# Layer norm computed in two halves, and the output bias moved from the norm into the attention

## The chip, the cores and the metric

The kernel runs on one core of a Trainium2 chip. The core has TensorE (PE: matmuls, weight loads shown apart as PEld), VectorE (DVE), ScalarE (ACT), GpSimd (POOL) and SyncE (SP, here DMA issues only). The metric is the device time of one execution in microseconds, as the median of several runs. A profile is one further execution.

## The reference, cut to what matters

Four layers work on x of 8 sequences x 256 tokens x 128 features. Each layer adds a gated cross attention and a gated feed-forward network, both fed by a layer norm of x:

```python
def _layernorm(x, axis=-1, eps=1e-05):
    m = jnp.mean(x, axis=axis, keepdims=True)
    v = jnp.var(x, axis=axis, keepdims=True)
    return (x - m) / jnp.sqrt(v + eps)
...
x = x + jnp.tanh(g_xattn[1]) * _L1_xattn_ref(_layernorm(x, axis=-1), ctx_768, L1_xattn_Wq, ..., L1_xattn_bo)
x = x + jnp.tanh(g_ffn[1]) * _L1_ffn_ref(_layernorm(x, axis=-1), L1_ffn_router_w, ...)
```

Every attention ends with `out @ Wo + bo`. So x receives, per layer, the gate times the attention's output and the gate times the bias `bo`. The norm in front reads x without either. Layer 0 has 16 heads of 8 features and a quantised feed-forward network, layers 1 and 3 have 16 heads of 64, layer 2 has 8 heads of 128 whose keys span all 2048 tokens, and layers 1 to 3 have expert networks with a router.

## The kernel before, in words

All 2048 tokens stay in SBUF as `x_res` (`M.x`): 128 partitions x 16 token tiles (`NT`) x 128 features. The program is a row of blocks. Each block gives every engine a list of instructions, and at a block's end all five engines meet at a barrier, so a block lasts as long as its slowest engine. Inside a block each engine works strictly in the written order and waits on semaphores; there is no scheduler and no planner.

The norm is a block of its own (`layernorm`, used six times: ahead of the four attentions and of the feed-forward networks of layers 0 and 3). The expert blocks of layers 1 and 2 (`sparse_ffn`) hold the same code at their start, so there are eight norms. In a norm

- DVE computes the statistics of the 16 tiles (L422, `BATCH_NORM_STATS2`), then seven small instructions on 128x16 numbers (L425 to L433) that end in variance plus epsilon, `ln_var_eps`;
- POOL raises this to the power -1/2 (L447, `ln_rstd`; L2291 in the expert blocks);
- DVE normalises the 16 tiles (L436; L2536 in the expert blocks), PE transposes each tile (L457), ACT copies four tiles at a time out of PSUM (L468, L470), and DVE forms the f16 remainder (L442, four instructions);
- ahead of an attention, POOL then adds the gated bias to all of `x_res` (L450) once all 16 tiles are normalised.

`attention` (layers 1 and 3) runs over 16 heads of 4 blocks of 512 queries. Heads 0 to 13 are a hardware loop of seven rounds, heads 14 and 15 are written out; the last one prepares no further head. Per block DVE does for each of two halves: reciprocal of the denominators (L1112), then two instructions that add the weighted output to `x_res` (L1122, the first waits for the reciprocal through the semaphore `rden_done`), and besides the remainders of the queries (L1088) and of the probabilities (L1128) and two maxima (L1098). PE writes both output halves (L969) into the same PSUM bank, so it writes the next one only when DVE has read the last. `attention_wide` (layer 2) does this with other tiles (L1516 adds to `x_res`; POOL shares the remainders of the probabilities, L1446, with DVE, L1494). In layer 0, `attention_small_heads` does not touch `x_res`; `gathered_projection` behind it does.

Of the kernel before, what the change touches and what calls it, by code (L numbers as in the profile page):

```python
# [28 lines left out]
P = 128  # L29
D = 128  # L30
# [26 lines left out]
def build(nc, d, out):  # L57
    with ExitStack() as ctx:
        M = persistent(nc, ctx)
        prepare(nc, M, d)  # L60
        for n in range(4):
            layernorm(nc, M, 2 * n, split=True, plain=False, bias=n)
# [10 lines left out]
            layernorm(nc, M, 2 * n + 1, split=n > 0, plain=True, bias=None)  # L73
# [326 lines left out]
def layernorm(nc, M, k, split, plain, bias):  # L400
# [4 lines left out]
    with ExitStack() as ctx:  # L405
# [8 lines left out]
        stat0 = seen * (NT + 5)  # L414
# [3 lines left out]
        with nc.Block() as block:  # L418
            @block.vector
            def _(dve):  # L420
                for t in range(NT):
                    nc.vector.bn_stats(st[:, t, :], M.x[:, t, :]).then_inc(s["stat"], 1)  # L422
                dve.wait_ge(s["stat"], stat0 + NT)

                nc.vector.tensor_tensor(a[:], st[:, :, 1], st[:, :, 4], ALU.add).then_inc(s["stat"], 1)  # L425
                nc.vector.tensor_tensor(b[:], st[:, :, 1], st[:, :, 4], ALU.subtract).then_inc(s["stat"], 1)
                nc.vector.tensor_tensor(c[:], st[:, :, 2], st[:, :, 5], ALU.add).then_inc(s["stat"], 1)
                dve.wait_ge(s["stat"], stat0 + NT + 3)
                nc.vector.tensor_scalar(mean[:], a[:], 0.5, None, ALU.mult)
                nc.vector.tensor_tensor(e[:], b[:], b[:], ALU.mult).then_inc(s["stat"], 1)  # L430
                nc.vector.tensor_scalar(c[:], c[:], 1.0 / D, EPS, ALU.mult, ALU.add).then_inc(s["stat"], 1)
                dve.wait_ge(s["stat"], stat0 + NT + 5)
# [41 lines left out]
def attention_small_heads(nc, M):  # L474
# [6 lines left out]
    with ExitStack() as ctx:  # L481
# [41 lines left out]
        with nc.Block() as block:  # L523
            @block.gpsimd
            def _(pool):
# [3 lines left out]
                nc.gpsimd.memset(empty[:, :, D:D + 1], 1.0e6).then_inc(empty_done, 1)  # L529

# [236 lines left out]
def attention(nc, M, layer):  # L767
# [90 lines left out]
    with ExitStack() as ctx:  # L858
# [37 lines left out]

        with nc.Block() as block:
# [178 lines left out]
            def _(pool):  # L1076
# [86 lines left out]
def attention_wide(nc, M, layer):  # L1163
# [9 lines left out]
    with ExitStack() as ctx:  # L1173
# [39 lines left out]

        with nc.Block() as block:
# [224 lines left out]
            def _(pool):  # L1439
                for r in (32, 96):  # L1440
                    nc.gpsimd.memset(K3[r:r + 1, :], 1.0).then_inc(ones_set, 1)

# [25 lines left out]
            def _(dve):  # L1468
# [41 lines left out]
                def add(b, half):  # L1510
                    qb = b % NQ
                    dve.wait_ge(o_ready, b + 1)
                    dve.wait_ge(rden_done, b + 1)
                    for t in (2 * half, 2 * half + 1):
# [655 lines left out]
def sparse_ffn(nc, M, d, layer):  # L2170
# [11 lines left out]
    with ExitStack() as ctx:  # L2182
# [66 lines left out]
        with nc.Block() as block:  # L2249
# [30 lines left out]
            def _(pool):  # L2280
# [9 lines left out]
                pool.wait_ge(var, 1)  # L2290
                nc.gpsimd.tensor_tensor(rstd[:], ve[:], M.neghalf[:], ALU.pow).then_inc(rstd_done, 1)  # L2291
# [472 lines left out]
```

## Time and profile before

| | |
|---|---|
| device time, median of 3 runs (lowest, highest) | 2480.14 us (2479.51, 2485.76) |
| device time of the profiled execution | 2482.54 us |
| its span, first to last instruction | 2480.8 us |
| busy: PE, DVE, ACT, POOL | 82%, 70%, 54%, 21% of the span |
| mean granted TensorE clock | 0.893 of full speed |

The profiled execution took 1.7 us more than its span; what is changed in the span is taken to change the device time by as much. Busy shares are averages over stages of different kinds: in a norm block the span is set by a chain through DVE and POOL, in the attentions by PE or DVE. The span of a chain is read from the timeline, by the start of one instruction and the start of the next that waits for it.

### The profile page before, as it was taken

The numbers are of one execution on the slowest core, as the hardware profiler recorded it, in microseconds if no ns is written. First come the engines' busy times: TensorE is split into PE (matmuls) and PEld (weight loads), VectorE is DVE, ScalarE is ACT, GpSimd is POOL, SyncE is SP. The second block draws the span as 40 slices with busy tenths as digits, with TensorE's granted clock in tenths as the row PEclk, the third lists the DMA queues.
The fourth block names the chain that finished last, engine by engine and source line by source line (L and its number), as shares of the span: only waits on it lengthen the run. The fifth ranks groups of instructions, "written<-read, shape, count | busy, mean of one in ns | idle before, by whom it ended". The sixth has DMA issues, their size and how long they took to land. (4 is left out here: it accounts for less than half of the span.)

```text
span 2480.8 us, 47937 instructions
## 1 busy us (share of the span) xinstructions
PE 2031.9 (82%) x17000; PEld 1395.1 (56%) x17001; DVE 1742.9 (70%) x3576; ACT 1339.0 (54%) x1775; POOL 531.4 (21%) x510
## 2 busy tenths in 40 slices
PE   3699636999984949999999999999547389999677
PEld 3434324888864715555555555556436268888544
DVE  2567365888875457788787877876535468888688
ACT  1247314777753416666666666667335257777321
POOL 2100001000002323434443344435433300000010
PEclk9679766999996959999999999999668689999789
DMA  5311100000004010000000000000211100000000
GB/s 143 57 24 11 23 0 1 0 0 0 0 27 120 19 49 9 9 12 9 12 9 11 11 9 12 9 11 4 84 54 40 40 1 0 0 0 0 1 22 24
DMA packets 94870, 53.74 MB, mean 22 GB/s; under 512 B 43517, under 2 KB 88808, under 8 KB 94358
## 3 DMA queue, kind: packets, MB, share of 16 engines
q1 hardware_dynamic: 86516, 42.51, 7.3%
q0 software_dynamic: 3584, 6.36, 0.8%
q10 hardware_dynamic: 4610, 2.71, 0.5%
q8 instruction: 104, 1.70, 0.3%
q14 instruction: 56, 0.46, 0.1%
HBM read 30.16 MB, written 13.75 MB: 18 GB/s over the span
## 5 line engine op out<-in xcount | busy, mean ns | idle before, releaser
L1446 POOL TENSOR_TENSOR aw_p_lo<-aw_p,aw_p_hi 128x512 f16<-128x512 f32 x256 | 303.1, 1184 | 499.6 <-ACT aw_p_hi L1400 499.5
L1482 DVE TENSOR_REDUCE aw_max_part<-ps 128x1 f32<-128x512 f32 x512 | 349.8, 686 | 77.2 <-PE ps L1275 74.4
L1398 ACT ACTIVATE aw_p<-ps 128x1024 f32<-128x1024 f32 x256 | 262.3, 1024 | 260.2 <-PE ps L1307 260.1
L1324 PE MATMUL ps<-ctx_hi_lo,aw_p_hi 128*128 128x194 f16 x2048 | 290.8, 247 | 1.2 <-DVE aw_p_lo L1494 0.7
L1494 DVE TENSOR_TENSOR aw_p_lo<-aw_p,aw_p_hi 128x512 f16<-128x512 f32 x256 | 267.5, 1045 | 22.0 <-ACT aw_p_hi L1400 22.0
L1327 PE MATMUL ps<-ctx_hi_lo,aw_p_lo 128*128 128x97 f16 x2048 | 279.4, 207 | 0.0
L1400 ACT ACTIVATE aw_p_hi<-ps 128x1024 f16<-128x1024 f32 x256 | 260.5, 1018 | 0.0
L1275 PE MATMUL ps<-ctxT_hi,aw_queries 96*128 96x512 f16 x512 | 204.1, 400 | 36.0 <-DVE aw_max_part L1482 35.4
L1327 PEld LDWEIGHTS ps<-ctx_hi_lo,aw_p_lo 128*128 128x128 f16 x2048 | 200.4, 98 | 26.1
L1324 PEld LDWEIGHTS ps<-ctx_hi_lo,aw_p_hi 128*128 128x128 f16 x2048 | 199.7, 98 | 5.0 <-issue 4.0
L1302 PE MATMUL ps<-aw_queries,aw_keys 128*128 128x512 f16 x512 | 194.5, 380 | 0.3 <-ACT aw_p_hi L1400 0.3
L1303 PE MATMUL ps<-aw_queries,aw_keys 128*128 128x512 f16 x512 | 193.9, 379 | 0.0
L1040 ACT ACTIVATE at_p<-ps 128x1024 f32<-128x1024 f32 x128 | 131.1, 1024 | 102.9 <-PE ps L946 102.9
L1098 DVE TENSOR_REDUCE at_neg_max<-ps 128x2 f16<-128x512 f32 x256 | 174.3, 681 | 6.0 <-PE ps L925 5.6
L1122 DVE SCALAR_TENSOR_TENSOR x_res<-ps,at_rden,x_res 128x128 f32<-128x128 f32 x520 | 158.6, 347 | 9.2
L447 POOL TENSOR_TENSOR ln_rstd<-ln_var_eps,neg_half 128x16 f32<-128x16 f32 x6 | 17.6, 2932 | 687.3 <-DVE ln_var_eps L433 653.2
L969 PE MATMUL ps<-C,u_out 97*128 (+1 forms) x1040 | 160.2, 276 | 5.1 <-DVE x_res L1122 5.1
L1128 DVE TENSOR_TENSOR at_p_lo<-at_p,at_p_hi 128x1024 f16<-128x1024 f32 x128 | 155.6, 1216 | 7.9 <-ACT at_p_hi L1042 7.7
L969 PEld LDWEIGHTS ps<-C,u_out 97*128 97x128 f32 x1040 | 136.2, 191 | 11.6 <-DVE x_res L1122 8.3
L956 PE MATMUL ps<-at_p_hi,ctx_hi_lo 128*128 128x256 f16 x512 | 140.9, 275 | 1.1 <-DVE at_p_lo L1128 1.1
L944 PE MATMUL ps<-at_q_hi,ctxT_hi 97*128 97x256 f16 x512 | 141.6, 277 | 0.0
L945 PE MATMUL ps<-at_q_hi,ctxT_lo 96*128 96x256 f16 x512 | 141.5, 276 | 0.0
(377 smaller groups left out, 4687.3 us busy)
## 6 DMA issues: line engine op xcount, KB each, us to landing
sf_weights_raw<-in_L_w SPq DMA_DIRECT2D x24, 256.0 KB, 4.1
slot_scratch<-at_empty_rows SPq DMA_DIRECT2D x16, 260.0 KB, 8.1
sf_fetched<-slot_scratch SPq DMA_DIRECT2D x16, 260.0 KB, 3.0
sf_weights_raw<-in_L_w SPq DMA_DIRECT2D x8, 512.0 KB, 3.8
x_norm<-result_scratch SPq DMA_DIRECT2D x8, 256.0 KB, 4.2
aw_queries<-aw_queries SPq DMA_DIRECT2D x32, 64.0 KB, 1.9
aw_queries<-aw_q_lo SPq DMA_DIRECT2D x32, 64.0 KB, 2.0
raw<-in_L_q SPq DMA_DIRECT2D x3, 512.0 KB, 10.4
```

The costliest lines, as they stand in the source:

```text
L969: ins = nc.tensor.matmul(ps[:, BANKS[b], t * (CW + 1):(t + 1) * (CW + 1)], M.U[:, upar, (2 * half + t) * P:(2 * half + t + 1) * P], C[:, s ...
L1098: nc.vector.tensor_reduce(nmax[:, par, 2 * k:2 * k + 2], ps[:, BANKS[b], :].rearrange("p (t k) -> p t k", t=2), AX.X, ALU.max, negate=True ...
L1275: nc.tensor.matmul(ps[:, bank, :], S1[0:DC, b % 4, t * P:(t + 1) * P], M.ct_hi[0:DC, kb * QB:(kb + 1) * QB], start=True, stop=True).then_i ...
L1302: nc.tensor.matmul(o, K1[:, ks], S1[:, c, :], start=True, stop=False)
L1303: nc.tensor.matmul(o, K2[:, ks], S2[:, c, :], start=False, stop=False)
L1324: nc.tensor.matmul(ps[:, bank, at:at + 2 * VW - 2], p_hi[:, n % 3, cols], M.cv[:, kt, 0:2 * VW - 2], start=kt == 0 and t % 2 == 0, stop=False,
L1327: ins = nc.tensor.matmul(ps[:, bank, at:at + DA], p_lo[:, n % 3, cols], M.cv[:, kt, 0:DA], start=False, stop=kt == NT - 1, skip_group_chec ...
L1398: nc.scalar.activation(p[:, n % 2, :].rearrange("p (b q) -> p b q", b=2), s, ACT.Exp, scale=1.0 / QS).then_inc(p_done, 1)
L1400: nc.scalar.activation(p_hi[:, n % 3, :].rearrange("p (b q) -> p b q", b=2), s, ACT.Exp, scale=1.0 / QS).then_inc(hi_done, 1)
L1446: nc.gpsimd.tensor_tensor(p_lo[:, n % 3, QB:], p[:, n % 2, QB:], p_hi[:, n % 3, QB:], ALU.subtract).then_inc(lo_b, 1)
L1482: nc.vector.tensor_reduce(mpart[:, b % 2, k:k + 1], ps[:, bank, :], AX.X, ALU.max).then_inc(m_done, 1)
L1494: nc.vector.tensor_tensor(p_lo[:, n % 3, 0:QB], p[:, n % 2, 0:QB], p_hi[:, n % 3, 0:QB], ALU.subtract).then_inc(lo_a, 1)
```

## The change

Three things change.

1. In every norm the 16 tiles are handled as two halves of 8 (`H = NT // 2`). DVE does statistics and the seven small instructions for tiles 0 to 7, then for tiles 8 to 15, and only then normalises; POOL computes the power in two instructions of 128x8 instead of one of 128x16, each as soon as its half's variance is there. The first 8 tiles are normalised after the first power, the others after the second.
2. The bias is no longer added in the norm. POOL adds it at the start of the attention that follows: in layer 0 behind its memsets, in layers 1 and 3 as POOL's only work, in layer 2 behind the memsets of the keys.
3. In layers 1 to 3 a new semaphore `bias_added` holds DVE's first addition to `x_res` back until the bias is in. The wait stands in the code of every such addition.

```diff
-def layernorm(nc, M, k, split, plain, bias):
+def layernorm(nc, M, k, split, plain):
...
+                for i in range(2):
+                    half, stats = slice(i * H, (i + 1) * H), stat0 + i * (H + 5)
+                    for t in range(i * H, (i + 1) * H):
+                        nc.vector.bn_stats(st[:, t, :], M.x[:, t, :]).then_inc(s["stat"], 1)
+                    dve.wait_ge(s["stat"], stats + H)
+                    nc.vector.tensor_tensor(a[:, half], st[:, half, 1], st[:, half, 4], ALU.add).then_inc(s["stat"], 1)
...
+                    nc.vector.scalar_tensor_tensor(ve[:, half], e[:, half], 0.25, c[:, half], ALU.mult, ALU.add
+                                                   ).then_inc(s["var"], 1)
                 for t in range(NT):
...
-                nc.vector.scalar_tensor_tensor(ve[:], e[:], 0.25, c[:], ALU.mult, ALU.add).then_inc(s["var"], 1)
-                dve.wait_ge(s["rstd"], seen + 1)
-                for t in range(NT):
+                    if t % H == 0:
+                        dve.wait_ge(s["rstd"], 2 * seen + t // H + 1)
                     nc.vector.tensor_scalar(M.xn[:, t, 0:D], M.x[:, t, :], mean[:, t:t + 1], rstd[:, t:t + 1],
                                             ALU.subtract, ALU.mult).then_inc(s["norm"], 1)
...
             def _(pool):
-                pool.wait_ge(s["var"], seen + 1)
-                nc.gpsimd.tensor_tensor(rstd[:], ve[:], M.neghalf[:], ALU.pow).then_inc(s["rstd"], 1)
-                if bias is not None:
-                    pool.wait_ge(s["norm"], (seen + 1) * NT)
-                    nc.gpsimd.tensor_tensor(M.x[:], M.x[:],
-                                            M.obias[:, bias:bias + 1, :].to_broadcast([P, NT, D]), ALU.add)
+                for i in range(2):
+                    half = slice(i * H, (i + 1) * H)
+                    pool.wait_ge(s["var"], 2 * seen + i + 1)
+                    nc.gpsimd.tensor_tensor(rstd[:, half], ve[:, half], M.neghalf[:, half], ALU.pow
+                                            ).then_inc(s["rstd"], 1)
...
@@ attention (layers 1 and 3), POOL and DVE @@
+                nc.gpsimd.tensor_tensor(M.x[:], M.x[:], M.obias[:, layer:layer + 1, :].to_broadcast([P, NT, D]),
+                                        ALU.add).then_inc(bias_added, 1)
...
                     v = ps[:, BANKS[at[0]], 0:2 * (CW + 1)].rearrange("p (t w) -> p t w", t=2)
+                    dve.wait_ge(bias_added, 1)
                     dve.wait_ge(rden_done, blk * 2 + half + 1)
```

`attention_wide` gets the same addition and the same wait (behind its two waits `o_ready` and `rden_done`), `attention_small_heads` the addition without a semaphore, and `sparse_ffn` the same two halves as `layernorm`.

The order of DVE's instructions in a norm, here the one of layer 0, before (`ln_` tiles belong to the norm, `ps` is PSUM; names in brackets are the semaphores an instruction waits for):

```order
L422 BN_STATS ln_stats<-x_res 128x6 x16
L425 TENSOR_TENSOR ln_a<-ln_stats 128x16 [waits ln_stat]
L426 TENSOR_TENSOR ln_b<-ln_stats 128x16
L427 TENSOR_TENSOR ln_c<-ln_stats 128x16
L429 TENSOR_SCALAR ln_mean<-ln_a 128x16 [waits ln_stat]
L430 TENSOR_TENSOR ln_e<-ln_b 128x16
L431 TENSOR_SCALAR ln_c<-ln_c 128x16
L433 SCALAR_TENSOR_TENSOR ln_var_eps<-ln_e,ln_c 128x16 [waits ln_stat]
L436 TENSOR_SCALAR x_norm<-x_res,ln_mean,ln_rstd 128x128 [waits ln_rstd]
L436 TENSOR_SCALAR x_norm<-x_res,ln_mean,ln_rstd 128x128 x15
L442 TENSOR_TENSOR x_normT_lo<-ps,x_normT_hi 128x512 [waits ln_hi] x4
```

The same place in the changed kernel, from the second half's statistics on (the first half's eight rows, which stand ahead, read the same as the first eight here):

```order
L424 BN_STATS ln_stats<-x_res 128x6 x8
L426 TENSOR_TENSOR ln_a<-ln_stats 128x8 [waits ln_stat]
L427 TENSOR_TENSOR ln_b<-ln_stats 128x8
L429 TENSOR_TENSOR ln_c<-ln_stats 128x8
L431 TENSOR_SCALAR ln_mean<-ln_a 128x8 [waits ln_stat]
L432 TENSOR_TENSOR ln_e<-ln_b 128x8
L433 TENSOR_SCALAR ln_c<-ln_c 128x8
L436 SCALAR_TENSOR_TENSOR ln_var_eps<-ln_e,ln_c 128x8 [waits ln_stat]
L441 TENSOR_SCALAR x_norm<-x_res,ln_mean,ln_rstd 128x128 [waits ln_rstd]
L441 TENSOR_SCALAR x_norm<-x_res,ln_mean,ln_rstd 128x128 x7
L441 TENSOR_SCALAR x_norm<-x_res,ln_mean,ln_rstd 128x128 [waits ln_rstd]
L441 TENSOR_SCALAR x_norm<-x_res,ln_mean,ln_rstd 128x128 x7
```

Between the first half's variance and the first normalisation DVE now has the second half's 15 instructions (8 of statistics, 7 small ones), and there is a second wait in the middle of the normalisation.

```order
L444 UNCONDITIONAL_BRANCH
L447 ISA
L447 TENSOR_TENSOR ln_rstd<-ln_var_eps,neg_half 128x16 [waits ln_var]
L450 TENSOR_TENSOR x_res<-x_res,out_bias 128x2048 [waits ln_norm]
L418 UNCONDITIONAL_BRANCH
L1075 UNCONDITIONAL_BRANCH [waits barrier_Pool_Activation_PE_DVE_SP_gather]
L897 UNCONDITIONAL_BRANCH
```

The same place in the changed kernel:

```order
L449 UNCONDITIONAL_BRANCH
L454 ISA
L454 TENSOR_TENSOR ln_rstd<-ln_var_eps,neg_half 128x8 [waits ln_var] x2
L418 UNCONDITIONAL_BRANCH
L1082 UNCONDITIONAL_BRANCH [waits barrier_Pool_Activation_PE_DVE_SP_gather]
L1089 TENSOR_TENSOR x_res<-x_res,out_bias 128x2048
L904 UNCONDITIONAL_BRANCH
```

The addition has moved from the norm's side of the barrier to the attention's side, and waits for nothing there.

DVE in the loop of the attention of layer 1, one half block and the query and maximum work behind it, before:

```order
L1112 RECIPROCAL at_rden<-ps 128x2 [waits at1_job_ready1]
L1122 SCALAR_TENSOR_TENSOR x_res<-ps,at_rden,x_res 128x128 [waits at1_rden_done]
L1122 SCALAR_TENSOR_TENSOR x_res<-ps,at_rden,x_res 128x128
L1086 REGISTER_ALU
L1088 TENSOR_TENSOR at_q_lo<-ps,at_q_hi 96x512 [waits at1_q_hi_done]
L1093 REGISTER_ALU
L1098 TENSOR_REDUCE at_neg_max<-ps 128x2 [waits at1_job_ready2]
```

The same place in the changed kernel:

```order
L1121 RECIPROCAL at_rden<-ps 128x2 [waits at1_job_ready1]
L1132 SCALAR_TENSOR_TENSOR x_res<-ps,at_rden,x_res 128x128 [waits at1_rden_done,at1_bias_added]
L1132 SCALAR_TENSOR_TENSOR x_res<-ps,at_rden,x_res 128x128
L1095 REGISTER_ALU
L1097 TENSOR_TENSOR at_q_lo<-ps,at_q_hi 96x512 [waits at1_q_hi_done]
L1102 REGISTER_ALU
L1107 TENSOR_REDUCE at_neg_max<-ps 128x2 [waits at1_job_ready2]
```

Nothing is reordered, but the first addition behind each reciprocal now has two waits. The wait for `rden_done` becomes an EVENT_SEMAPHORE of its own between the reciprocal and the addition.

## Rows read from the trace of the kernel before

**Rows 1.** The page: span, then busy us, share and instructions by engine.

```profile
span 2480.8 us, 47937 instructions
PE 2031.9 (82%) x17000; PEld 1395.1 (56%) x17001; DVE 1742.9 (70%) x3576; ACT 1339.0 (54%) x1775; POOL 531.4 (21%) x510
```

**Rows 2.** Busy time in layer 3's attention: length; PE, PEld, DVE, ACT, POOL; clock; DMA.

```profile
2007.00:2329.00 322.00, 317.74 (x2700) 262.06 (x2698) 281.11 (x634) 230.81 (x310) 0.00 (x0) 1.00 0.00 0
```

**Rows 3.** Timeline, norm of layer 0: start, length (us), engine, line, what, count, [idle before<-releaser].

```profile
90.48 3.19 DVE L422 BATCH_NORM_STATS2 ln_stats<-x_res 128x6 f32<-128x128 f32 x16 [0.30 <-PEq L193]
...
94.48 0.18 DVE L433 SCALAR_TENSOR_TENSOR ln_var_eps<-ln_e,ln_c 128x16 f32<-128x16 f32 x1
94.74 2.94 POOL L447 TENSOR_TENSOR ln_rstd<-ln_var_eps,neg_half 128x16 f32<-128x16 f32 x1 [75.50 <-DVE ln_var_eps L433]
97.72 4.19 DVE L436 TENSOR_SCALAR x_norm<-x_res,ln_mean,ln_rstd 128x128 f32<-128x128 f32 x16 [3.06 <-POOL ln_rstd L447]
...
101.84 2.47 DVE L442 TENSOR_TENSOR x_normT_lo<-ps,x_normT_hi 128x512 f16<-128x512 f32 x4
102.00 4.50 POOL L450 TENSOR_TENSOR x_res<-x_res,out_bias 128x2048 f32<-128x2048 f32 x1 [4.31 <-DVE x_norm L436]
...
106.82 0.59 PE L556 MATMUL ps<-ctxT_hi,w0k_hi 97*128 97x512 f16 x1 [4.38 <-PEq L418]
```

**Rows 4.** Two lines' instructions: ns min/median/max, first and last start.

```profile
L447 POOL TENSOR_TENSOR ln_rstd<-ln_var_eps,neg_half x6: 2912/2937/2947, 94.7 to 2333.3; 128x16 f32<-128x16 f32 x6
...
L450 POOL TENSOR_TENSOR x_res<-x_res,out_bias x4: 4495/4496/4497, 102.0 to 1973.6; 128x2048 f32<-128x2048 f32 x4
```

**Rows 5.** Timeline, the norm ahead of the attention of layer 1.

```profile
373.22 2.95 POOL L447 TENSOR_TENSOR ln_rstd<-ln_var_eps,neg_half 128x16 f32<-128x16 f32 x1 [34.11 <-issue]
376.20 4.20 DVE L436 TENSOR_SCALAR x_norm<-x_res,ln_mean,ln_rstd 128x128 f32<-128x128 f32 x16 [6.75 <-POOL ln_rstd L447]
```

**Rows 6.** Timeline, layer 1's expert block: its power and the first scatter of tokens.

```profile
739.90 2.92 POOL L2291 TENSOR_TENSOR sf_rstd<-sf_var_eps,neg_half 128x16 f32<-128x16 f32 x1 [2.95 <-DVE sf_var_eps L2533]
...
760.78 1.30 POOL L2297 DMA_INDIRECT slot_scratch<-x_norm,sf_slot_at  x1 [17.97 <-DVE sf_slot_at L2607]
```

**Rows 7.** Timeline, layer 2's attention: POOL and DVE on SBUF tiles together.

```profile
957.30 1.16 POOL L1446 TENSOR_TENSOR aw_p_lo<-aw_p,aw_p_hi 128x512 f16<-128x512 f32 x1 [2.25 <-ACT aw_p_hi L1400]
957.45 1.56 DVE L1494 TENSOR_TENSOR aw_p_lo<-aw_p,aw_p_hi 128x512 f16<-128x512 f32 x1
```

**Rows 8.** Timeline, layer 0's quantised network: one scaling over 2048 columns.

```profile
317.13 1.29 DVE L1665 TENSOR_SCALAR qf_tmp<-x_normT,qf_inv_x 128x2048 f32<-128x2048 f32 x1
```

**Rows 9.** Timeline, one block near the end of layer 1's attention.

```profile
703.51 0.17 DVE L1112 RECIPROCAL at_rden<-ps 128x2 f32<-128x2 f32 x1 [0.34 <-PE ps L969]
...
703.72 0.61 DVE L1122 SCALAR_TENSOR_TENSOR x_res<-ps,at_rden,x_res 128x128 f32<-128x128 f32 x2
...
704.24 1.22 DVE L1128 TENSOR_TENSOR at_p_lo<-at_p,at_p_hi 128x1024 f16<-128x1024 f32 x1
...
704.50 0.52 PEld L969 LDWEIGHTS ps<-C,u_out 97*128 97x128 f32 x4
```

**Rows 10.** Waits from 420 to 710 us: us in total, times, longest.

```profile
DVE at_rden L1112 <- PE ps L969: 15.6, 58, 0.3
```

**Rows 11.** Timeline of DVE where layer 1's attention ends (unrolled, L1107's wait between).

```profile
715.46 0.68 DVE L1098 TENSOR_REDUCE at_neg_max<-ps 128x2 f16<-128x512 f32 x1
716.29 0.17 DVE L1112 RECIPROCAL at_rden<-ps 128x2 f32<-128x2 f32 x1
716.49 0.61 DVE L1122 SCALAR_TENSOR_TENSOR x_res<-ps,at_rden,x_res 128x128 f32<-128x128 f32 x2
```

**Rows 12.** Timeline, last additions of layer 3's attention.

```profile
2326.49 0.61 DVE L1122 SCALAR_TENSOR_TENSOR x_res<-ps,at_rden,x_res 128x128 f32<-128x128 f32 x2
2327.15 0.71 PE L969 MATMUL ps<-C,u_out 97*128 97x129 f32 x4 [0.91 <-DVE x_res L1122]
```

**Rows 13.** Timeline of DVE: the first addition to x in layer 1's attention.

```profile
416.19 0.61 DVE L1122 SCALAR_TENSOR_TENSOR x_res<-ps,at_rden,x_res 128x128 f32<-128x128 f32 x2
```

More of the change, by code:

```diff
@@ L61, in build @@
         for n in range(4):
-            layernorm(nc, M, 2 * n, split=True, plain=False, bias=n)
+            layernorm(nc, M, 2 * n, split=True, plain=False)
             if n == 0:
@@ L72, in build @@
                 continue
-            layernorm(nc, M, 2 * n + 1, split=n > 0, plain=True, bias=None)
+            layernorm(nc, M, 2 * n + 1, split=n > 0, plain=True)
             if n == 0:
@@ L413, in layernorm @@
         M.norms += 1
-        stat0 = seen * (NT + 5)
+        stat0, H = seen * (NT + 10), NT // 2
         splits0 = M.splits
@@ L434, in _ @@
-                dve.wait_ge(s["rstd"], seen + 1)
-                for t in range(NT):
+                for i in range(2):
[4 more added lines that the diff above has]
+                    nc.vector.tensor_tensor(a[:, half], st[:, half, 1], st[:, half, 4], ALU.add).then_inc(s["stat"], 1)
+                    nc.vector.tensor_tensor(b[:, half], st[:, half, 1], st[:, half, 4], ALU.subtract
+                                            ).then_inc(s["stat"], 1)
+                    nc.vector.tensor_tensor(c[:, half], st[:, half, 2], st[:, half, 5], ALU.add).then_inc(s["stat"], 1)
+                    dve.wait_ge(s["stat"], stats + H + 3)
+                    nc.vector.tensor_scalar(mean[:, half], a[:, half], 0.5, None, ALU.mult)
+                    nc.vector.tensor_tensor(e[:, half], b[:, half], b[:, half], ALU.mult).then_inc(s["stat"], 1)
+                    nc.vector.tensor_scalar(c[:, half], c[:, half], 1.0 / D, EPS, ALU.mult, ALU.add
+                                            ).then_inc(s["stat"], 1)
+                    dve.wait_ge(s["stat"], stats + H + 5)
+                    nc.vector.scalar_tensor_tensor(ve[:, half], e[:, half], 0.25, c[:, half], ALU.mult, ALU.add
+                                                   ).then_inc(s["var"], 1)
@@ L1212, in is_unit @@
             return 0 <= n < NU
+        bias_added = sem("bias_added")
         with nc.Block() as block:
@@ L1441, in _ @@
                     nc.gpsimd.memset(K3[r:r + 1, :], 1.0).then_inc(ones_set, 1)
+                pool.wait_ge(ones_set, 2)
+                nc.gpsimd.tensor_tensor(M.x[:], M.x[:], M.obias[:, layer:layer + 1, :].to_broadcast([P, NT, D]),
+                                        ALU.add).then_inc(bias_added, 1)
                 def lows(n):
@@ L2289, in _ @@
                                    allow_small_or_imprecise_dtypes=True).then_inc(consts, 1)
-                pool.wait_ge(var, 1)
-                nc.gpsimd.tensor_tensor(rstd[:], ve[:], M.neghalf[:], ALU.pow).then_inc(rstd_done, 1)
+                for i in range(2):
+                    half = slice(i * NT // 2, (i + 1) * NT // 2)
+                    pool.wait_ge(var, i + 1)
+                    nc.gpsimd.tensor_tensor(rstd[:, half], ve[:, half], M.neghalf[:, half], ALU.pow
+                                            ).then_inc(rstd_done, 1)
                 for k in range(K):
@@ L2529, in _ @@
-                V.tensor_scalar(mean[:], a[:], 0.5, None, ALU.mult)
-                V.tensor_tensor(e2[:], b[:], b[:], ALU.mult).then_inc(stat, 1)
-                V.tensor_scalar(c[:], c[:], 1.0 / D, EPS, ALU.mult, ALU.add).then_inc(stat, 1)
-                dve.wait_ge(stat, NT + 5)
-                V.scalar_tensor_tensor(ve[:], e2[:], 0.25, c[:], ALU.mult, ALU.add).then_inc(var, 1)
-                dve.wait_ge(rstd_done, 1)
-                for t in range(NT):
+                H = NT // 2
+                for i in range(2):
+                    half, stats = slice(i * H, (i + 1) * H), i * (H + 5)
+                    for t in range(i * H, (i + 1) * H):
+                        V.bn_stats(st[:, t, :], M.x[:, t, :]).then_inc(stat, 1)
+                    dve.wait_ge(stat, stats + H)
+                    V.tensor_tensor(a[:, half], st[:, half, 1], st[:, half, 4], ALU.add).then_inc(stat, 1)
+                    V.tensor_tensor(b[:, half], st[:, half, 1], st[:, half, 4], ALU.subtract).then_inc(stat, 1)
+                    V.tensor_tensor(c[:, half], st[:, half, 2], st[:, half, 5], ALU.add).then_inc(stat, 1)
+                    dve.wait_ge(stat, stats + H + 3)
+                    V.tensor_scalar(mean[:, half], a[:, half], 0.5, None, ALU.mult)
+                    V.tensor_tensor(e2[:, half], b[:, half], b[:, half], ALU.mult).then_inc(stat, 1)
+                    V.tensor_scalar(c[:, half], c[:, half], 1.0 / D, EPS, ALU.mult, ALU.add).then_inc(stat, 1)
+                    dve.wait_ge(stat, stats + H + 5)
+                    V.scalar_tensor_tensor(ve[:, half], e2[:, half], 0.25, c[:, half], ALU.mult, ALU.add
+                                           ).then_inc(var, 1)
```

22 lines of the change are left out of this document (6 added, 16 removed).

## The prediction

> **What bounds the kernel now.** I read the page first, for the shares, then the timeline of each norm block, then busy time by stretch and the timeline in the attentions that get a new wait. No engine bounds the whole: PE is busy 82%, DVE 70%, POOL 21% [rows 1]. So every edit is priced in its own stage.
>
> In a norm block the end is set by one chain. In layer 0 [rows 3]: DVE's statistics start at 90.48 and end at 93.67; seven small instructions end with the variance at 94.66; POOL's power runs from 94.74 to 97.68 with DVE idle (3.06 us); DVE normalises from 97.72 to 101.91; the remainders end at 104.31. Then only POOL works: its bias addition, held back until the last tile is normalised, runs from 102.00 to 106.50, and the next block's first matmul follows at 106.82. Two costs are to be seen there: an exposed power of 2.94 us, and 106.50 - 104.31 = 2.19 us in which all engines wait for the addition. Power and addition last the same everywhere, 2937 and 4496 ns in the median [rows 4].
>
> In the attentions of layers 1 and 3 PE is the bound: 317.7 us busy of 322 at full granted clock [rows 2]. A block repeats every 5.04 us, and DVE waits for PE in each, 15.6 us in 58 blocks or 0.27 us a block [rows 10].
>
> **The change, part by part.**
>
> Bias out of the norm. Four norms had it. Each block now ends with DVE: 4 x 2.19 = 8.8 us gained. The additions go into the attentions. In layer 1 the norm's work ends 6.7 us (4.2 + 2.5) after 376.20, the barrier takes about 0.5, so POOL adds from about 383.4 to 387.9; DVE's first addition to x comes at 416.19 [rows 5, 13], 28 us later, so the new wait holds nothing back. Nor should the addition slow DVE: beside it in the norm, four remainders (one input from PSUM, one from SBUF) took 2.47 us, 0.62 each [rows 3], and DVE's work at an attention's start reads PSUM too. Bounds: 0, or 4.5 us for each of the four were DVE held for all of it; I take 0. POOL has nothing urgent behind the addition.
>
> The new wait. In layers 1 and 3 there are 16 x 4 + 1 = 65 pairs of output halves, so 130 times per layer the wait for the reciprocal becomes an EVENT_SEMAPHORE ahead of the addition. The trace has this pattern ahead of L1112: the maximum ends at 716.14, the reciprocal starts at 716.29, 0.15 us later; with the wait carried by the instruction itself the gap is 716.46 to 716.49, 0.03 [rows 11]. So it costs 0.11 us. Not below 0, since it waits for what was waited for before; up to 0.15. In the steady blocks there is cover for just that. The additions end at 704.33 and PE's next weight load for that bank starts at 704.50 [rows 9], while where PE does wait for the additions it follows 0.05 behind (2327.10 to 2327.15) [rows 12]: slack 0.12 against 0.11. Over a block DVE loses 0.22 against its idle 0.27. So the loop stays at 5.04. If the cover fails, each 0.01 us beyond it costs 60 x 2 x 0.01 = 1.2 us. In the last head DVE and PE hand one bank to and fro [rows 12], and the wait shows: of its last ten projections I count seven on the chain, 7 x 2 x 0.11 = 1.5 us lost (0 to 20 x 0.11 = 2.2). In layer 2 each first addition had two waits already, so no sequencer instruction is added: 0, at most 64 x 0.11 = 7.
>
> Two halves. The power of 8 columns is not in the trace. Bounds: half of 2.94, or all of it. POOL's subtraction of 512 columns takes 1.16 us [rows 7] and its addition of 2048 takes 4.50 [rows 4], 2.17 ns a column and 0.05 fixed, so POOL is paid by the column: 0.05 + 2.89 / 2 = 1.50. The halved statistics take 1.6 us, the small instructions 1.0 as before, since at 128x16 they are all start-up. In layer 0's times: first variance 93.1, first power 93.2 to 94.7, second statistics and variance done at 95.7, second power wants 95.8 to 97.3, and DVE can normalise from 95.7. With nothing in its way it ends at 95.7 + 4.19 = 99.9 instead of 101.91: 2.0 us gained.
>
> But then the second power runs beside the normalisation. The rows nearest to that: POOL's subtraction from 957.30 to 958.46, DVE's from 957.45 to 959.01, 1.56 us for what would take 0.61 by the 1.22 of twice the size [rows 7, 9]. DVE came second and ended 0.55 after POOL: it had stood still. Does the normalisation, with one tensor input, use what they compete for? Scaling 2048 columns within SBUF took 1.29 us [rows 8], 0.63 ns a column, where DVE's subtraction with two inputs takes 1.22 for 1024 [rows 9], 1.19 ns. It takes two columns at a time, so I read it as using the second way in and out too. Then the first tile goes 95.7 to 96.0, the power to 97.5, fifteen tiles 97.5 + 14 x 0.26 + 0.34 = 101.4: 0.5 gained. If DVE holds POOL off instead, the eight tiles end at 97.8, the power at 99.3, and the other eight at 101.5: the same. I take 0.5 of 0.5 to 2.0, the rows nearest saying so. The statistics go at one column a time and are not held. Seven norms: 7 x 0.5 = 3.5 us. In the expert blocks it passes on, since the first scatter at 760.78 hangs on the norm through DVE [rows 6]. The eighth, ahead of layer 1's attention, differs: its power starts at 373.22 for a reason that is POOL's own ("issue", where layer 0's row names DVE), and DVE stands idle for 6.75 us [rows 3, 5]. There the powers end at 374.7 and 376.2; DVE, held by the second, starts at 376.25 instead of 376.20: 0, or 1.45 gained if it isn't held.
>
> The Trainium skill has this as a rule (SBUF — State Buffer, "Who interferes with whom"): a VectorE `tensor_scalar` in a two-port mode, or an instruction with two SBUF inputs against a GpSimd one that reads SBUF, excludes GpSimd's instruction for its whole length, and whoever comes first blocks the other. By that rule each norm gains 0.5; without it 2.0. The trace agrees for two inputs (the 1.56 us); for the normalisation no row shows it.
>
> **Sum.** -8.8 (barrier) - 3.5 (halves) + 1.5 (last heads) = -10.8 us. The profiled execution is 2482.54 with 1.7 outside its span, so 2471.7 for one like it; the median of the runs shown is 2.4 lower, and that is what is compared: 2480.1 - 10.8 = 2469.
>
> **Rivals.**
>
> Not held: the power and the normalisation run side by side. -8.8 - 7 x 2.0 - 1.45 + 1.5 = -22.7: 2457. For it: POOL's power reads and writes only 8 columns in 1.5 us, so it could leave the way free for most of that. Against: the one collision shown was a full stop [rows 7].
>
> The power is paid by the instruction, and it holds DVE. With p its time, DVE's small instructions with two SBUF inputs at 94.7 also stand until 93.2 + p, the norm ends at 98.4 + 2p, which is 2p - 3.5 worse than now, and layer 1's 2p - 2.95. With the -7.3 of the rest the total is 16p - 34.7, above zero from p = 2.2; at 2.94 it is +12.3: 2492. For it: only one width is in the trace. Against: POOL's other work goes by the column.
>
> The loop's cover fails: the wait costs 0.17 instead of 0.11, by 0.05 over the slack in 120 blocks: 6 us, and 0.8 more in the last heads: 2476. For it: 0.01 us between slack and cost. Against: every steady block shows the same slack and the pattern measured is the same one.
>
> The change does nothing: the norm isn't on the path. Excluded by [rows 3]: PE starts the next block 0.3 us behind POOL.
>
> **How the numbers follow.** Forecast 0.50 (2465 to 2473), not held 0.32, cover fails 0.11, power by the instruction 0.07. A measurement here tells 0.3%, 7.4 us, from no change, so below 2472.7 is faster. Forecast 0.46 of 0.50, not held 0.32, cover fails 0.03: faster 0.81. The rest of these, 0.04 and 0.08, is the same, and slower is 0.07. The range reaches over the not-held case with 2 us for its rounding, and to the failed cover: 2455 to 2476.
>
> **What would show it.** The norm blocks: next block's first matmul within 0.5 us of DVE's last remainder; layer 0's block from 90.48 to 106.82, 16.3 us, to be 13.6. POOL's power 1.50. DVE's 16 normalisations stretched from 4.19 to about 5.7 if held, 4.2 if not. In the attention's blocks the reciprocal's end and the addition's start 0.15 apart; blocks still 5.04; DVE's wait for PE down from 0.27 to 0.05. Wrong if powers last near 2.9, if the blocks lengthen, or if the first addition to x waits for POOL.

## The result and the profile after

The changed kernel takes 2458.34 us (median of 4 runs, 2453.95 to 2461.74) where the kernel before, on the same chip, takes 2480.38 (4 runs): ratio 0.9908, 95% interval 0.9888 to 0.9928, so 22.0 us less. The forecast was 2469, 11 us less; the measured time is close to that of the rival "not held", 2457.

The page of the profiled execution, 2461.74 us long, answers to [rows 1]:

```profile
span 2460.0 us, 48265 instructions
PE 2037.3 (83%) x17001; PEld 1399.2 (57%) x17001; DVE 1749.1 (71%) x3632; ACT 1338.8 (54%) x1775; POOL 535.5 (22%) x518
```

The timeline of layer 0's norm answers to [rows 3]:

```profile
90.14 1.65 DVE L424 BATCH_NORM_STATS2 ln_stats<-x_res 128x6 f32<-128x128 f32 x8 [0.30 <-PEq L193]
...
92.63 1.63 DVE L424 BATCH_NORM_STATS2 ln_stats<-x_res 128x6 f32<-128x128 f32 x8
92.79 1.68 POOL L454 TENSOR_TENSOR ln_rstd<-ln_var_eps,neg_half 128x8 f32<-128x8 f32 x1 [73.56 <-DVE ln_var_eps L436]
...
95.02 0.17 DVE L436 SCALAR_TENSOR_TENSOR ln_var_eps<-ln_e,ln_c 128x8 f32<-128x8 f32 x1
95.11 4.19 DVE L441 TENSOR_SCALAR x_norm<-x_res,ln_mean,ln_rstd 128x128 f32<-128x128 f32 x16
95.27 1.76 POOL L454 TENSOR_TENSOR ln_rstd<-ln_var_eps,neg_half 128x8 f32<-128x8 f32 x1 [0.80 <-DVE ln_var_eps L436]
...
99.21 2.48 DVE L447 TENSOR_TENSOR x_normT_lo<-ps,x_normT_hi 128x512 f16<-128x512 f32 x4
...
101.99 0.59 PE L562 MATMUL ps<-ctxT_hi,w0k_hi 97*128 97x512 f16 x1 [2.17 <-PEq L418]
```

VectorE's row for the normalisation has no idle time ahead of it, and its sixteen instructions take 4.19 us, as before, with a power running beside the first eight of them. Here and below, the end of a norm is the end of its last normalisation: it comes 9.16 us after the norm's start instead of 11.43, 2.27 us earlier. The next block's first matmul starts 11.85 us after the norm's start instead of 16.34: the other 2.2 us are the bias addition that is gone from the end.

The powers answer to [rows 4] (ns min/median/max, first and last start):

```profile
L454 POOL TENSOR_TENSOR ln_rstd<-ln_var_eps,neg_half x12: 1628/1677/1857, 92.8 to 2314.9; 128x8 f32<-128x8 f32 x12
```

Layer 1's norm, the one whose power comes late [rows 5], and GpSimd's bias addition behind it:

```profile
364.80 3.31 POOL L454 TENSOR_TENSOR ln_rstd<-ln_var_eps,neg_half 128x8 f32<-128x8 f32 x2 [33.55 <-issue]
366.52 4.20 DVE L441 TENSOR_SCALAR x_norm<-x_res,ln_mean,ln_rstd 128x128 f32<-128x128 f32 x16 [4.53 <-POOL ln_rstd L454]
...
373.79 4.50 POOL L1089 TENSOR_TENSOR x_res<-x_res,out_bias 128x2048 f32<-128x2048 f32 x1 [5.68 <-SPq L904]
```

The addition is over at 378.3; the first addition to x follows at 403.99, 26 us later [rows 13]. Nor does the addition slow VectorE: from the block's first matmul to the first addition to x layer 1's attention takes 30.4 us, before 30.7. Layer 3's attention ends so, with the doubled wait at L1129 between two of its rows [rows 11, 12]:

```profile
2306.88 0.17 DVE L1121 RECIPROCAL at_rden<-ps 128x2 f32<-128x2 f32 x1 [0.80 <-PE ps L976]
2307.15 0.61 DVE L1132 SCALAR_TENSOR_TENSOR x_res<-ps,at_rden,x_res 128x128 f32<-128x128 f32 x2
```

The addition starts 0.10 us behind the end of the reciprocal, and 0.27 behind its start. Read from the records of all 130 pairs of a layer to the nanosecond, the gap is 104 ns, before 35: the wait costs 0.069 us. In the steady blocks TensorE's next load follows the additions by 0.105 us where it was 0.174, and blocks still last 5.04. Where TensorE does wait for them it follows by 0.052.

Stage by stage, from one norm's start to the next (us):

```
                 before    after    change   the norm's own end
to first norm     90.48    90.14    -0.3
layer 0, attn    206.99   201.77    -5.2     11.44 to 9.16
layer 0, ffn      67.80    65.02    -2.8     11.41 to 9.17
layer 1, attn    370.37   367.93    -2.4     15.14 to 13.79
layer 1, exp.    149.33   146.69    -2.6     11.42 to 9.17
layer 2, attn    869.12   866.26    -2.9     11.43 to 9.16
layer 2, exp.    208.06   208.78    +0.7     11.41 to 9.30
layer 3, attn    366.92   363.18    -3.7     11.44 to 9.44
the rest         151.78   150.25    -1.5     11.40 to 9.17
```

The eight norms sum to -16.7. Layer 3's ends 0.28 us later than layer 0's: its first power starts 3.53 us after the norm's start, not 2.65, and VectorE waits for it. Why GpSimd starts it late isn't shown.

```profile
1951.83 4.19 DVE L441 TENSOR_SCALAR x_norm<-x_res,ln_mean,ln_rstd 128x128 f32<-128x128 f32 x16 [0.18 <-POOL ln_rstd L454]
```

One stage went the wrong way, layer 2's experts. Its norm gave 2.1 us; the router's 32 matmuls behind it took them back. First before, then after:

```profile
1765.70 4.16 PE L2319 MATMUL ps<-sf_router_w,x_normT 128*128 128x8 f32 x32
```

```profile
1747.43 6.83 PE L2337 MATMUL ps<-sf_router_w,x_normT 128*128 128x8 f32 x32
```

The stretch around them (length, then busy us of PE, PEld, DVE, ACT, POOL, granted clock, DMA), before and after:

```profile
1766.00:1770.00 4.00, 3.86 (x30) 3.76 (x30) 3.11 (x7) 2.57 (x5) 0.00 (x0) 0.83 0.46 133
```

```profile
1748.00:1753.00 5.00, 5.00 (x25) 5.00 (x25) 2.80 (x5) 2.34 (x5) 0.00 (x0) 0.50 0.57 158
```

It is the clock: 0.50 is 1.2 GHz, 0.83 a stretch mostly at 2.4. The experiments say whether the change did that.

### The profile page after: what moved, and what is told of

It reads as the page before. It is cut to its first block and busy times, and to the rows that moved or that the text cites. A ratio compares the mean times of both kernels' runs of the same rounds, so it can differ in the third digit from the quotient of the medians.

```text
span 2460.0 us, 48265 instructions
## 1 busy us (share of the span) xinstructions
PE 2037.3 (83%) x17001; PEld 1399.2 (57%) x17001; DVE 1749.1 (71%) x3632; ACT 1338.8 (54%) x1775; POOL 535.5 (22%) x518
## 5 line engine op out<-in xcount | busy, mean ns | idle before, releaser
L1107 DVE TENSOR_REDUCE at_neg_max<-ps 128x2 f16<-128x512 f32 x256 | 174.4, 681 | 6.0 <-PE ps L932 5.6
L454 POOL TENSOR_TENSOR ln_rstd<-ln_var_eps,neg_half 128x8 f32<-128x8 f32 x12 | 20.6, 1716 | 672.8 <-DVE ln_var_eps L436 639.2
## 6 DMA issues: line engine op xcount, KB each, us to landing
raw<-in_L_q SPq DMA_DIRECT2D x3, 512.0 KB, 10.4
```

Source lines behind the costliest of these rows:

```text
L1107: nc.vector.tensor_reduce(nmax[:, par, 2 * k:2 * k + 2], ps[:, BANKS[b], :].rearrange("p (t k) -> p t k", t=2), AX.X, ALU.max, negate=True ...
```

## The experiments

They ran on three chips, each beside the kernel before, whose medians there were 2483.2, 2489.9 and 2485.8 us; so ratios to it are compared, not times. The intervals are some 0.2% (5 us) either way, and the traces decide below that.

**The whole again, and its two parts apart.**

The changed kernel again: 

> The changed kernel once more, beside the parts of it. Expected 2454 to 2462 us, about 22 us under the kernel before. One profile showed 2460.0 us of span, and the three others 2452 to 2460: the theory is that the 6 us between them are stages whose granted clock falls differently, above all the router product of layer 2's expert block (12 us after that block's start), which ran at half clock in the profile of after and at full clock in the one of before. If so, the stages other than that one repeat to within 0.5 us.

Measured 0.9904 (0.9881 to 0.9926), 6 runs from 2451.48 to 2465.41. Its stages repeat those of the first profile within 0.25 us in four of nine and within 1.5 us in four more, but layer 0's attention took 194.96 us instead of 201.77. The clock of its profile and of the first, in the same stretch:

```profile
148.00:164.00 16.00, 15.74 (x179) 7.51 (x174) 12.03 (x20) 12.61 (x17) 0.00 (x0) 0.99 0.07 6
```

```profile
148.00:164.00 16.00, 15.77 (x112) 6.36 (x107) 7.20 (x13) 8.05 (x10) 0.00 (x0) 0.55 0.00 2
```

PE is busy for 15.7 us in both, and does 179 matmuls in the one and 112 in the other. The router's matmuls took 6.84 here. So executions of one kernel differ by where the clock rises. I had named the wrong stage as the one that varies: between these two it is mainly this one, and three of the others miss the expected 0.5 us too.

The bias alone: 

> The bias leaves the norm and goes into the attentions, the norm stays in one piece. Theory A (the additions were worth 2.19 us in each of four norms, and the doubled wait costs 0.069 us, 8 times on the chain of each of two last heads): -8.8 + 1.1 = -7.7 us, 2472.5. Rival (the halves gave only the 3.5 us forecast and the rest of the 22 came with the bias): about -18 us, 2462.

```
-                for i in range(2):
+                for i in range(1):
```

(so for the statistics and for the power of every norm: one piece, all else as changed).

Measured 0.9958 (0.9941 to 0.9975), -10.4 us by that ratio: theory A's -7.7 lies in the interval, the rival's -18 outside it. In layer 0 the norm ends at 11.45 as before, and the next matmul comes 2.2 us earlier, as the addition used to end 2.19 behind VectorE.

The halves alone: 

> The norm in halves, the bias addition still in the norm by GpSimd after the last tile. Theory A (nothing is held, each norm gains 2.27 us, seven of them, and 1.35 in layer 1): -17.2 us, 2463, the block with the bias still ends with GpSimd's addition, 2.3 us behind DVE. Rival (normalisation held by the second power): -3.5 us, 2477.

```
+                if bias is not None:
+                    pool.wait_ge(s["norm"], (seen + 1) * NT)
+                    nc.gpsimd.tensor_tensor(M.x[:], M.x[:], M.obias[...], ALU.add)
...
-                nc.gpsimd.tensor_tensor(M.x[:], M.x[:], M.obias[...], ALU.add).then_inc(bias_added, 1)
-                    dve.wait_ge(bias_added, 1)
```

Measured 0.9948 (0.9932 to 0.9965), -12.9 us. The norms end at 9.16 to 9.44, layer 1's at 13.82, and sum to -16.8. The rival's 0.9986 is excluded. Theory A's 0.9931 lies just outside the interval too, 4 us from the ratio. It is the norms in the trace that bear theory A out, not the time. The two parts add up to -23.3 and the whole gave -23.8, so no interaction is seen; with 4 or 5 us of doubt in each, that the sums are so close is partly luck.

**Does the power hold VectorE?** The first three of these kernels ran once each, so their traces are read and their times are not compared.

GpSimd's subtraction beside the normalisation: 

> The changed kernel with one more GpSimd instruction in each of six norms: behind the second power a subtraction of two SBUF tiles, 512 columns, whose result nobody reads. It runs beside VectorE's tiles 8 to 12. Theory P (the normalisation uses the way into SBUF that it shares with GpSimd, and the power only left it free because it moves 8 columns in 1.65 us): one of the two stands still while the other runs, so the 16 normalisations stretch from 4.19 to 4.7 to 5.4 us, or the subtraction lasts 1.7 to 3 us instead of 1.16. Theory Q (the normalisation, with one tensor input, doesn't use it at all): 4.19 and 1.16, and the end of the norm block doesn't move.

```
+                nc.gpsimd.tensor_tensor(junk[:], M.x[:, 0:4, :], M.x[:, 4:8, :], ALU.subtract)
```

Layer 0's norm, and then all sixteens (ns min/median/max):

```profile
95.54 5.24 DVE L442 TENSOR_SCALAR x_norm<-x_res,ln_mean,ln_rstd 128x128 f32<-128x128 f32 x16
...
95.70 1.85 POOL L455 TENSOR_TENSOR ln_rstd<-ln_var_eps,neg_half 128x8 f32<-128x8 f32 x1 [0.80 <-DVE ln_var_eps L437]
97.35 1.29 POOL L457 TENSOR_TENSOR ln_junk<-x_res 128x512 f32<-128x512 f32 x1
```

```profile
L442 DVE TENSOR_SCALAR x_norm<-x_res,ln_mean,ln_rstd x96: 332/343/1400, 95.5 to 2331.6; 128x128 f32<-128x128 f32 x96
```

One normalisation in each of the six norms lasts 1.4 us instead of 0.34: it stood for 1.05 us, nearly the whole of GpSimd's 1.29. Theory P: the normalisation does use the way that the two engines share. My reading of its rate (0.63 ns a column, [rows 8]) was right.

VectorE's subtractions beside the power: 

> The changed kernel with two more VectorE instructions in each of six norms, subtractions of two SBUF tiles of 512 columns ahead of the normalisation, whose results nobody reads: the first starts with the second power, the second lies wholly beside it. Theory P (the power leaves the shared way free): 0.61 to 0.7 us each, the power 1.65 to 1.9, each norm block 1.25 us longer, so 7.5 us in six norms. Theory Q (it is the normalisation that doesn't use the way, and the power holds an instruction with two inputs): the second subtraction ends with the power, up to 1.7 us long, or the power starts late and ends after 97.8.

```
+                for j in range(2):
+                    nc.vector.tensor_tensor(junk[:, 4 * j:4 * j + 4, :], M.x[:, 0:4, :], M.x[:, 4:8, :], ALU.subtract)
```

```profile
L440 DVE TENSOR_TENSOR ln_junk<-x_res x12: 684/686/691, 95.0 to 2322.4; 128x512 f32<-128x512 f32 x12
```

```profile
L457 POOL TENSOR_TENSOR ln_rstd<-ln_var_eps,neg_half x12: 1632/1682/2022, 92.7 to 2322.0; 128x8 f32<-128x8 f32 x12
```

An instruction that surely uses the shared way (two SBUF inputs, held for 0.95 us in [rows 7]) isn't held by the power. Ten of the twelve run beside one; the two of layer 1, where the power comes later, run alone and took 684 and 686 ns, and all twelve lie within 7 ns. It is the power that pays, up to 0.37 us.

A wide power: 

> The changed kernel with a third power of 32 columns in each of six norms, with a result that nobody reads, wholly beside VectorE's tiles 8 to 15. Its own time by the line above: 0.36 + 32 x 0.161 = 5.5 us. Theory P (a power moves its few columns quickly and spends its time computing, so it leaves the shared way free at any width): the 16 normalisations stay at 4.19 to 4.3 us. Rival (the power was too small to be seen, and a wider one holds VectorE like the subtraction of 512 columns did, which made 5.24 of 4.19): normalisations stretch by 0.5 us or more.

```
+                nc.gpsimd.tensor_tensor(junk[:], ones[:], M.obias[:, 0, 0:32], ALU.pow)
```

```profile
97.16 5.45 POOL L459 TENSOR_TENSOR ln_junk<-ln_ones,out_bias 128x32 f32<-128x32 f32 x1
```

```profile
95.35 4.22 DVE L442 TENSOR_SCALAR x_norm<-x_res,ln_mean,ln_rstd 128x128 f32<-128x128 f32 x16
```

5.45 us as worked out, and the normalisations 4.22. A power four times as wide leaves the way free for nearly all of its time as well.

Nearly, and not wholly. The single normalisations (ns min/median/max), in the kernel before, where no power runs beside them, and in the changed kernel:

```profile
L436 DVE TENSOR_SCALAR x_norm<-x_res,ln_mean,ln_rstd x96: 333/341/348, 97.7 to 2340.1; 128x128 f32<-128x128 f32 x96
```

```profile
L441 DVE TENSOR_SCALAR x_norm<-x_res,ln_mean,ln_rstd x96: 334/344/388, 95.1 to 2318.6; 128x128 f32<-128x128 f32 x96
```

By the records of the changed kernel, one normalisation lasts 372 to 388 ns in three of the eight norms, the one under way when the second power ends, and that power lasts 1.63 to 1.67 us. In the other five no normalisation is longer than 351 ns, and the second power lasts 1.76 to 1.86. With the wide power, in three norms of six the normalisation that follows its start comes 0.04 us late (295 to 298 ns after the one before, where 256 is usual). So the two engines do meet for a moment at a power's start or end, and either VectorE pays, at most 0.05 us, or the power does, up to 0.2. A power behaves as if it took the way only while its columns move.

GpSimd normalising four tiles: 

> The changed kernel with GpSimd normalising the last 4 of 16 tiles in six norms, behind its second power, beside VectorE's tiles. If neither holds the other, VectorE ends 12 tiles at 8.1 us of the block and GpSimd its four at 8.2 (0.33 us each by 2.17 ns a column) instead of 9.16: 1.0 us a norm, 6 us in all. If they exclude each other (theory P of the run with GpSimd's subtraction), the two together take as long as before or longer: 0 to +6 us.

```
-                for t in range(NT):
+                for t in range(NT - 4):
...
+                for t in range(NT - 4, NT):
+                    nc.gpsimd.tensor_scalar(M.xn[:, t, 0:D], M.x[:, t, :], mean[:, t:t + 1], rstd[:, t:t + 1],
+                                            ALU.subtract, ALU.mult).then_inc(s["norm2"], 1)
```

```profile
L458 POOL TENSOR_SCALAR x_norm<-x_res,ln_mean,ln_rstd x24: 787/808/1296, 97.4 to 2329.6; 128x128 f32<-128x128 f32 x24
```

Measured 0.9914 (0.9897 to 0.9931), no gain. Neither excludes the other for a whole instruction (VectorE's twelve end at 8.19 us, its slowest 0.44 us; GpSimd's first tile of a norm takes 0.86 to 1.30 where one alone takes 0.79), but GpSimd needs 0.81 us a tile in the median, not 0.33, and ends at 10.4 where the changed kernel's norm ends at 9.16. The price that I carried over from a two-input operation was wrong for this one.

**How the parts of the norm are priced.** Quarters: 

> The norm in four quarters instead of halves. The power: by 2.94 us at 16 columns and 1.65 at 8 it goes as 0.36 + 0.161 a column, so 1.0 us at 4 columns (rival: a floor near 1.65). VectorE never waited for it in halves, so no power is left to hide, and two more sets of seven small instructions, 0.84 us each, are added: norm blocks 1.7 us longer, eight of them, so +13 us against the changed kernel, about 2471. Rival (DVE's small instructions are hidden behind something else): 0.

```
-                for i in range(2):
+                for i in range(4):
```

```profile
L455 POOL TENSOR_TENSOR ln_rstd<-ln_var_eps,neg_half x24: 996/1018/1133, 92.7 to 2331.2; 128x4 f32<-128x4 f32 x24
```

Measured 0.9963 (0.9949 to 0.9977), some 15 us over the changed kernel's ratio (0.9904, on another chip); 13 expected. The norms end at 10.90 instead of 9.16, 1.74 each, though layer 1's only 0.25. With 2.94, 1.65, 1.02 and 5.45 us at 16, 8, 4 and 32 columns the power is 0.37 us and 0.16 a column. (The expectation's "VectorE never waited for it in halves" is not so in layers 1 and 3, as shown above.)

**The doubled wait.** One wait ahead of the heads: 

> The changed kernel with the wait for the bias once ahead of the heads instead of ahead of each addition. Theory A (0.069 us a wait, shown only where PE waits for the additions): the gap between reciprocal and addition goes from 0.104 back to 0.035, PE's slack in a block from 0.105 to 0.174, the last heads lose 0.55 us less each, so -1.1 us against the changed kernel run beside it. Rival (the wait also lengthens the turn of each head, 7 turns by 0.03 to 0.07 in layer 1): -1.5 to -2. Rival (nothing, the register's wait is not what cost): 0.

```
-                    dve.wait_ge(bias_added, 1)
                     dve.wait_ge(rden_done, blk * 2 + half + 1)
...
                 lows(0, 0)
+                dve.wait_ge(bias_added, 1)
                 each_head(dve, head)
```

Measured 0.9890 (0.9870 to 0.9910) against 0.9904 on the same chip, which the intervals don't tell apart. The traces do: the gap is back at 35 ns, TensorE's load at 0.173 behind. Layer 1's attention takes 366.08 us instead of 367.93 and 368.03, layer 3's 362.52 instead of 363.18 and 363.21. From reciprocal to reciprocal, the last head gives 0.61 us back in each layer. So do the turns between the loop's seven rounds, 0.38 and 0.32 us in layer 1 and 0.22 in layer 3. The rest of layer 1's difference, 0.9 and 1.0 us, lies in its norm, ahead of the loop and at the end of the block, and differently in the two profiles of the changed kernel, so it isn't put down to the wait.

More waits: 

> The changed kernel with four more waits, all long met, ahead of each addition to x in layers 1 and 3, which become two more sequencer instructions there. Theory A (each costs 0.069 us, and in a steady block only 0.053 us of cover is left: PE's load follows the additions at 0.105, and never closer than 0.052): the gap between reciprocal and addition 0.24, PE waits for the first addition of a block, blocks last 5.04 + 0.085 = 5.13 us, so 60 x 2 x 0.085 = 10 us, and 8 x 2 x 0.138 = 2.2 us in the last heads: 12 us over the changed kernel, about 2470. Rival (the blocks aren't sensitive to the waits at all, only the last heads): +2.2 us, blocks stay 5.04.

```
                     dve.wait_ge(bias_added, 1)
+                    dve.wait_ge(qhi_done, 1)
+                    dve.wait_ge(nmax_done, 1)
+                    dve.wait_ge(exp_done, 1)
+                    dve.wait_ge(u_evac, 1)
```

Measured 0.9915 (0.9895 to 0.9935), 2.7 us over the changed kernel's ratio, where theory A said 12 and the rival 2.2; the intervals exclude the first alone. Read to the nanosecond the gap is 133, not 240. The trace has three sequencer instructions ahead of the addition, but in all but two of the 260 places the first two start, and end, while the reciprocal is still busy. Only the third stands in the gap. It waits for two semaphores and lasts 50 ns, where the changed kernel's waits for one and lasts 21 (first that one, then the third; ns min/median/max):

```profile
L1129 DVEq EVENT_SEMAPHORE  x260: 21/21/21, 403.9 to 2308.8; - x130
```

```profile
L1133 DVEq EVENT_SEMAPHORE  x260: 49/50/50, 405.9 to 2315.6; - x130
```

These 29 ns are the whole of what the four waits add. TensorE follows at 0.077, still above its nearest 0.052, and blocks last 5.04. So theory A's price a wait fell, and whether blocks grow once the cover is gone was not reached.

**Is the low clock behind the norms the change's?** Matmuls in the norm's idle time: 

> The changed kernel with 40 matmuls of 128 columns in PE's idle time ahead of the transposes in each of the eight norms; their results are never read. Theory A (the granted clock stands at half after a norm because PE idles in it for 6 us, and part of what the shorter norm gives is lost as stages run longer at the low clock): the stages behind the norms get the full clock earlier, the router product of layer 2's expert block in 5.1 us instead of 10, in all 10 us less or more. Rival (the clock of a stage hangs on its own work, not on 6 us of the norm): same stage lengths within 0.5 us, 0 us.

```
+                for _ in range(40):
+                    nc.tensor.matmul(M.ps[:, 7, 0:P], M.ident16[:], M.ident16[:], start=True, stop=True)
```

Measured 0.9909 (0.9897 to 0.9922), no gain. The matmuls at layer 2's experts, the router's last:

```profile
1733.90 3.96 PE L2330 MATMUL ps<-ident 128*128 128x128 f16 x40 [1.48 <-PEq L1227]
1739.40 4.33 PE L2333 MATMUL ps<-ident,x_norm 128*128 128x128 f32 x16 [1.53 <-DVE x_norm L2563]
1743.53 6.62 PE L2341 MATMUL ps<-sf_router_w,x_normT 128*128 128x8 f32 x31
```

The router's stay at the low clock. Over the profiles, this product took 4.1 to 4.4 us in before and in five of the others (the halves alone, VectorE's subtractions, GpSimd's tiles, the wide power, the early power), all with halved norms, and 6.6 to 6.8 in the rest, the bias alone with its undivided norms among them. So neither level goes with the change. Theory A fell; what sets the clock in one execution stays open.

**The late power of layer 1, and the best version.** 

> The version with one wait for the bias, and besides one power of a single column on GpSimd right behind the second all-reduce of layer 0's quantised network. Theory L (in layer 1's norm GpSimd's first power waits 5.2 us, until 7.87 us into the block, because after the all-reduces it has to load something before its next ordinary instruction; done early that is hidden): the power starts at 2.65 us, the norm ends at 9.17 instead of 13.8, and 4.6 us are gained against the version with one wait: ratio to the kernel before about 0.987. Rival (the delay hangs on the new block or on the time since GpSimd last worked): 0, the power still starts near 7.8.

```
                 nc.gpsimd.partition_all_reduce(hall[:], hm[:], P, RMAX).then_inc(hmax_all, 1)
+                pool.wait_ge(xmax_all, 1)
+                nc.gpsimd.tensor_tensor(early[:], mall[:], M.neghalf[:, 0:1], ALU.pow)
```

In the changed kernel GpSimd's queue has a configuration ahead of this power, 6.9 us before it starts:

```profile
L454 POOLq MODIFY_POOL_CONFIG  x2: 11/11/11, 357.9 to 357.9; - x2
```

With one power early, GpSimd's timeline is:

```profile
329.49 0.37 POOL L1664 PARTITION_ALL_REDUCE qf_hmax_all<-qf_hmax  x1 [22.50 <-DVE qf_hmax L1695]
336.64 1.47 POOL L1666 TENSOR_TENSOR qf_early<-qf_max_all,neg_half 128x1 f32<-128x1 f32 x1 [6.78 <-issue]
359.53 1.66 POOL L454 TENSOR_TENSOR ln_rstd<-ln_var_eps,neg_half 128x8 f32<-128x8 f32 x1 [21.42 <-DVE ln_var_eps L436]
```

The 6.78 us now lie in the network's shadow, the norm's power starts at 2.65 and layer 1's norm ends at 9.16 instead of 13.60 us. The rival falls: GpSimd has been idle for 21 us and the block is new, and yet the power starts at once. The early power took 1.47 us for a single column, far more than the line above gives (0.53); why isn't shown. Measured 0.9867 (0.9843 to 0.9891): theory L, and the lowest ratio of all, 2453.7 us where before took 2485.8. Layer 1's norm is 4.4 us shorter than in the version with one wait (0.9890); the two ratios the intervals don't tell apart.

The Trainium skill (GPSIMD Engine Reference, "Instruction dispatch") says that the first call to a freshly loaded GpSimd kernel additionally pays some 6 us for loading it. The trace agrees in size: 6.78 us here, and 6.9 from the configuration to the power in the changed kernel.

## Why the prediction was wrong

- **The failed step: "I take 0.5 of 0.5 to 2.0"** for the halves of a norm, because the second power would stop the normalisation. Seven norms gave 2.00 to 2.28 each, 15.4 in all, and layer 1's 1.35; forecast were 3.5 and 0. That is 13.2 us, more than the whole miss of 11. Of its two premises one was right: the normalisation shares a way with GpSimd (1.4 instead of 0.34 us beside the subtraction). The other was not: that a power occupies it while it runs. I took the price of a collision from [rows 7], a subtraction that moves 512 columns in 1.16 us, and put it on an instruction that moves 8 in 1.65. What the runs showed in its place: VectorE loses 0.05 us at most beside a power, of 8 or of 32 columns. The rival's reason, that so few columns could leave the way free, stood in the text with 0.32.
- **The rule of the Trainium skill** (SBUF — State Buffer, "Who interferes with whom"), by which the one that comes first blocks the other for its whole length, gave 0.5 a norm. The traces agree with it for the subtraction (1.05 us lost) and disagree for the power (0.05 at most) and for GpSimd's own normalisation (0.10); the measurement decides.
- **The power's length** of 1.50 was 1.65 alone and up to 1.86 beside the normalisation: my line through the additions had 0.05 fixed, the power has 0.37. In layer 0 it was hidden either way: the first ended 0.6 us before VectorE wanted it, the second 0.2 before the ninth tile. Only where GpSimd began late did VectorE wait, 0.18 us in layer 3 and 4.53 in layer 1.
- **The bias, -8.8**, was right: the next matmul follows the norm's end 2.2 us sooner in each of the four, and nothing waits for the bias later.
- **The wait, +1.5**, was right in size by two errors. A wait costs 0.069, not 0.11; a last head loses 0.61 us, which is nine of them and not seven; and the turns between rounds, which I had not counted, lose 0.6 in both layers together: 1.8 in all. The loop stayed at 5.04, with 0.053 us of cover left where I saw 0.01.
- **The sum with these sizes**: -16.7 - 8.8 + 1.8 = -23.7. Measured -22.0 by the first medians and -23.8 by the second. The profiled pair shows -20.8 in the spans. The 2.7 us of the router's product at the low clock are nearly the difference, and belong to the execution, not to the change; but layer 0's attention alone differs by 6.8 us between two executions, so that it comes out so closely is luck.
- The rivals that the power is paid by the instruction and that the loop's cover fails are both refuted (1.68 us at 8 columns where 16 take 2.94; blocks of 5.04).

## What to carry to other kernels

Here two engines that share a way into memory collided by what they moved, not by how long an instruction lasted: price an overlap from a row of the same operation, and where there is none, let a slow, narrow one weigh towards no collision. A step of 3 us between two engines that one of them waits out was worth halving; quartering it cost more in small instructions (0.87 us a set) than was left to hide. Behind an all-reduce on GpSimd, its next ordinary instruction paid 6.8 us: issue a small one at once, where nobody waits.

## What was not expected of the hardware

- A sequencer instruction between two dependent VectorE ones costs 69 ns when it waits for one semaphore and 98 when it waits for two; two more ahead of it, whose waits are long met, run while VectorE is still busy and cost nothing.
- GpSimd's normalisation (two operations, two values per partition) takes 0.81 us for 128 columns, 6.3 ns each, where its two-input addition takes 2.2.
- The granted clock of the same stretch of the same kernel was 0.99 in one execution and 0.55 in another, and layer 0's attention, which it is part of, differed by 6.8 us; a difference of one profile under 7 us needs a second profile or the stage's clock before it is explained.
